# Pieces of eight steps for the read weights, and a doubled planning time for the projections

## The reference

```
xr, gate = split(x @ W_in.T)                    # 1024 + 1024 wide
xc = silu(conv4(xr + t_emb) + b_conv)           # causal, depthwise, 4 taps
xn = layernorm(xc)
Bm, Cm, dt = split(xn @ W_xproj.T, 3)           # 16 + 16 + 16
Ad = 1 + 0.01 * tanh(dt @ W_dt.T + b_dt) * A
Bd = Bm * min(norm(xn), 1)
h  = clip(h * Ad + Bd * xn, -10, 10)            # 16 states x 1024, one step per token
y  = Cm . h + D * xn
out = x + (y * silu(gate)) @ W_out.T
```

## Time and profile before

| what | us |
|---|---|
| median of 3 runs | 6659.12 |
| lowest, highest | 6656.98, 6682.08 |
| profiled execution, its own time | 6651.31 |
| its span from first to last instruction | 6649.5 |
| first `q` to last `q` of the 1024 steps | 3607.1 to 6530.2 |

### The profile page before, as it was taken

The page is one execution under the profiler, slowest core; times in us unless marked ns, Lnnn a source line. Parts: engine busy times, 40 slices in busy tenths (PEclk is TensorE's granted clock), DMA queues, the critical chain, the costliest instruction groups (busy, mean ns, idle before and its releaser), DMA issues. The chain is left out here.

```text
span 6649.5 us, 73076 instructions
## 1 busy us (share of the span) xinstructions
PE 6031.6 (91%) x24000; PEld 2737.8 (41%) x24000; DVE 4565.5 (69%) x5830; ACT 2368.7 (36%) x4476; POOL 3213.6 (48%) x2625
## 2 busy tenths in 40 slices
PE   8999999999999999999965779999999999999997
PEld 4444444444444444444332324444343434444343
DVE  4655655555555556555425988989888888989882
ACT  2444434444444444444524313233232323333110
POOL 1776765767567566665715223424243333424212
PEclk8999999999999999999977989999999999999998
DMA  2223223232231322312123333434344443534433
GB/s 89 79 80 90 86 65 90 66 105 73 73 96 50 108 82 71 99 46 89 41 101 98 79 92 93 134 85 133 97 114 122 111 122 92 136 85 130 104 88 99
DMA packets 411563, 613.28 MB, mean 92 GB/s; under 512 B 58768, under 2 KB 189968, under 8 KB 410672
## 3 DMA queue, kind: packets, MB, share of 16 engines
q1 hardware_dynamic: 374320, 558.24, 30.4%
q10 hardware_dynamic: 36864, 50.38, 3.0%
HBM read 305.31 MB, written 201.38 MB: 76 GB/s over the span
## 5 line engine op out<-in xcount | busy, mean ns | idle before, releaser
L1103 POOL TENSOR_TENSOR acc<-acc,prob 128x512 f32<-128x512 f32 x1536 | 1906.6, 1275 | 960.9 <-PE bank L793 740.8
L1033 DVE TENSOR_REDUCE mx<-bank 128x1 f32<-128x512 f32 x2048 | 1314.9, 684 | 587.1 <-PE bank L763 582.5
L1907 DVE SCALAR_TENSOR_TENSOR g<-xps,bd,g 128x1024 f32<-128x1024 f32 x1024 | 1313.5, 1283 | 236.9 <-PE xps L1669 157.2
L926 ACT ACTIVATE prob<-misc 128x512 f32<-128x512 f32 x1496 | 842.5, 597 | 849.5 <-PE misc L780 688.3
L1669 PE MATMUL xps<-sx,spread 128*128 128x512 f32 x2048 | 899.1, 524 | 249.2 <-DVE g L1907 233.2
L763 PE MATMUL bank<-khat,qhat 96*128 96x512 f32 x2048 | 989.3, 534 | 39.6 <-DVE mx L1033 20.7
L1913 DVE TENSOR_SCALAR g<-g,lim 128x1024 f32<-128x1024 f32 x1024 | 876.3, 856 | 30.0
L780 PE MATMUL misc<-qhat,khat 98*128 98x512 f32 x1679 | 723.9, 461 | 58.4 <-ACT prob L926 42.1
L1669 PEld LDWEIGHTS xps<-sx,spread 128*128 128x128 f32 x2048 | 354.7, 193 | 808.6 <-DVE g L1907 472.1
L1683 PE MATMUL yps<-g,cexp 128*32 128x512 f32 x4096 | 618.7, 631 | 1.2 <-DVE g L1913 0.8
L763 PEld LDWEIGHTS bank<-khat,qhat 96*128 96x128 f32 x2048 | 390.5, 196 | 435.0 <-issue 300.3
(11 more groups left out here) (199 smaller groups left out, 6740.5 us busy)
## 6 DMA issues: line engine op xcount, KB each, us to landing
sx<-scratch_xhl SPq DMA_DIRECT2D x512, 128.0 KB, 5.0
scratch_dx<-dx SPq DMA_DIRECT2D x64, 512.0 KB, 3.0
scratch_xhl<-xhi SPq DMA_DIRECT2D x64, 512.0 KB, 4.6
scratch_xhl<-xn SPq DMA_DIRECT2D x64, 512.0 KB, 4.9
scratch_y<-ysb SPq DMA_DIRECT2D x512, 64.0 KB
dx_t<-scratch_dx SPq DMA_DIRECT2D x59, 512.0 KB, 6.2
y_t<-scratch_y SPq DMA_DIRECT2D x59, 512.0 KB, 4.3
xt_n<-in_x SPq DMA_DIRECT2D x112, 256.0 KB, 2.9
```

Source lines behind the costliest of these rows:

```text
L926: act.activation(to, bank[m][:, 0:QC], ACT.Exp, scale=SCALE).then_inc(sem[f"act_m{m}"], 1)
L1033: dve.tensor_reduce(self.mx2[:, h * TT + qt, c:c + 1], bank[m][:, 0:QC], AX.X, ALU.max).then_inc(sem[f"dve_m{m}"], 1)
L1103: pool.tensor_tensor(self.acc[:, a, h, :], self.acc[:, a, h, :], self.prob[:, (n % 2) * GH + h, :], ALU.add).then_inc(sem["pool_acc"], 1)
L1907: dve.scalar_tensor_tensor(self.g[:, t % 4, :], self.xps[t % 2][:, :], self.bd[:, i % 2, tl:tl + 1], self.g[:, (t - 1) % 4, :], ALU.mult, ...
```

## The change

It has two parts.

Read weights: `out` waits for the piece of eight steps it reads rather than the last piece of the half. A piece is made once the `out` that last read those eight steps has gone. The planner sees 0.65 for a piece and no longer 0.8. Only the first piece of a chunk stays at the end of the rows' lane; the other fifteen have a lane of their own, due from 4 steps ahead of the chunk to 0.84 of it.

Projections: the planner believes 0.9 instead of 0.47 for half a batch's projection.

```diff
-    def expand(i, h):
-        done = (("out", (i - 1) * TOK + (h + 1) * HC - 2),) if i else ()
-        return [item("POOL", 0.8, ("ex", i, h, a), (("d3", i),) + done, [("pool_ex", 1)], port=True) for a in range(HC // 8)]
+    def expand(i, some):
+
+        done = lambda k: (("out", (i - 1) * TOK + 8 * k + 6),) if i else ()
+        return [item("POOL", 0.65, ("ex", i, 8 * k // HC, k % (HC // 8)), (("d3", i),) + done(k), [("pool_ex", 1)], port=True)
+                for k in some]
...
-                    put("PE", 0.47, ("pj", i, hb, bb, q), (("silu", i, hb, CT - 1),), [("pe_m{m}", 1)] if q else [],
+                    put("PE", 0.9, ("pj", i, hb, bb, q), (("silu", i, hb, CT - 1),), [("pe_m{m}", 1)] if q else [],
...
-        return out + expand(i, 0)
+        return out + expand(i, range(1))
...
-                put(t, "PE", 1.0, ("out", t - 1), (("g", t),) + ((("ex", i, h, HC // 8 - 1),) if tl % HC == 1 else ()) + (
+                put(t, "PE", 1.0, ("out", t - 1), (("g", t),) + ((("ex", i, h, tl % HC // 8),) if tl % 8 == 1 else ()) + (
...
-        order.lane(expand(i, 1), t - 1.0, t + 0.25 * TOK)
+        order.lane(expand(i, range(1, TOK // 8)), t - 4.0, t + 0.84 * TOK)
...
-                w.wait_ge(sem["pool_ex"], plan.after("pool_ex", ("ex", t // TOK, t % TOK // self.HC, self.HC // 8 - 1)))
+                w.wait_ge(sem["pool_ex"], plan.after("pool_ex", ("ex", t // TOK, t % TOK // self.HC, t % self.HC // 8)))
...
-                    w.wait_ge(sem["pe_y"], plan.after("pe_y", ("out", (i - 1) * self.TOK + (h + 1) * self.HC - 2)))
+                    w.wait_ge(sem["pe_y"], plan.after("pe_y", ("out", (i - 1) * self.TOK + h * self.HC + 8 * a + 6)))
```

## The result

The changed kernel takes 6680.64 us (median of 20 runs, 6665.93 to 6689.27); the kernel before takes 6659.24 in 20 runs beside it. The ratio is 1.003, 95% interval [1.0023, 1.0037]: slower by 0.3%, a difference that so many runs do tell from none. The forecast was 6631, faster by 28, in a range of 6590 to 6685.

The account below looks back on a forecast made before the run. VectorE and PE alternate in a ring; time can be won only where VectorE idles and PE can feed it. 6651.31 (profiled) - 28 = 6623, that execution being 7.8 us under the median, so 6631; range 6590 to 6685.

Parts of the forecast that it names:

- Part 1a: At steps 39 to 43 and 80 to 82 of a chunk: truer projection time removes waits of `pjo`, 28 us gained.
- Rival 1: At both `pjo` places PE is the limit; waits only move from `proj` to `xps`: 6659, no change, chance 0.23.
- Part 1b: What else the 0.9 moves in the convolution's lane (items due up to 3.5% earlier): nothing, between -6 and +6 us.
- Part 2a: Waits of `out` for read weights, now for one piece: the old wait was always met, so 0.
- Part 2b: Moving the pieces on GpSimd: later rows and possible collisions with `g`, taken as 0, bounds -5 to +54 us.
- Its two mechanisms: Rows' chain ending about 9 us later, under 12 us of cover; late unpaced items colliding with `g`, 0.92 us each.
- rival 3: At the chunk's head the rows' chain becomes the bound, with nine unpaced collisions: 6698, slower, chance 0.15.
- Rival 2: Near the projections the plan is now true and all direct and following waits go: 6591, chance 0.15.
- `pjo` under 10, `xps` up by less than 30, chunks of 370 to 373, `g` at 856: Signs the forecast is right: `pjo`'s wait from 50.3, `q`'s for `xps` from 157.2, chunk times in us, mean `g` in ns.
- wrong if chunks get over 377: Sign that the prediction is wrong: chunks of the changed stage take over 377 us.

Follow-up runs that it names:

- e_dur65: The changed kernel with the convolution's lane ending at 0.65 of the chunk instead of 0.62 and due steps weighted as for 0.47: 6622.7 us, ratio 0.9937.
- e_proj: The kernel before with only the projections' believed time raised from 0.47 to 0.9: 6684.3 us, ratio 1.0044.
- e_wait_only: The kernel before with only the waits of the change, every engine's order kept: 6658.7 us, ratio 0.9997.
- e_read: The changed kernel with the projections' believed time put back to 0.47, leaving only the read weights' part: 6677.4 us, ratio 1.0029.

## Why the prediction was wrong

**Part 1a, taken as a gain of 28 us, is the step that failed.** It read the earlier trace rows as slack: `pjo` waits, no `q` near it does, so TensorE "has the inputs ready". The rows of TensorE at the same steps, which I had not set beside them, were gapless. In the order of before, halving the projections returned all of the 49 us taken away, at both places alike. The direct waits stayed in the changed kernel (53.5), and the claim that the false belief of 0.47 is what makes them was wrong: with the 0.9 VectorE meets the same queue. Where they did go (1.7 us in `e_dur65`), the time did not. Rival 1 named this mechanism and I gave it 0.23; it gave 6659, and misses the rest.

**Part 1b, costed at nothing between -6 and +6, is the missing term.** I bounded the reshuffle by the scatter of chunk lengths, in which the clock of TensorE hardly varied (6.8 to 20.5 us low in each of the six). The 0.9 moved the first projections 7 to 9 us ahead in chunks 1 to 6 (13.9 to 4.6 in the calm one), behind steps in which TensorE idles, and there the clock falls for longer. `e_proj` alone costs 25 us by the medians, and most of it goes with the clock. That the place of the projections is what lengthens the stretches rests on where they begin and on the clocks of the kernels with and without the wider due steps; no run moved the projections and nothing else. No sentence of the prediction looked at the granted clock, though it stood in the rows.

**Part 2a held.** The waits give 0 (`e_wait_only`, 0.9997).

**Part 2b, taken as 0, cost 18 us alone**, inside the bounds of -5 to +54. Its two mechanisms don't carry it. The chain of rows did not become late, and collisions fell over the stage (-8 us in `e_read`), though they rose by 6 us in the last steps of the chunks, so rival 3 did not happen. The cost stands in TensorE's waits (+14 us idle) and those of `q` for `xps` (+28), and in a low stretch of chunk 0. The loss in steps 96 to 126 is the part that every kernel with moved pieces pays (11 us in `e_read`). With the lane's end at 0.65 the pieces and the duration together cost 4 us (`e_dur65`), as other steps give time back.

The two costs do not add up. Alone they are 18 and 25 us, together 21, so behind the moved pieces the 0.9 cost 3 us more (6680.6 against 6677.4, less than these runs can tell).

**Rival 2** (all waits go, 6591) fell with 1a. The lists of signs did their work: of "`pjo` under 10, `xps` up by less than 30, chunks of 370 to 373, `g` at 856" the first and third failed; and "wrong if chunks get over 377" came true in two.

**Open:** why a stretch begins 4 us behind the `q` of step 34 in one chunk and 6 in the next, which decides between 17.1 and 3.4 us; how much of the 10 us that chunk 0 of `e_read` lost is the clock; why the gate's load comes late at step 109; and whether the 14 us by the line through the runs is all cause, since slower runs could also make the clock lower.

## What to carry to other kernels

A wait of a reader for a matmul is slack only if TensorE has a gap before it; set the two timelines side by side before a wait is counted as gain. When an order is moved, compare TensorE's busy time for the same number of instructions. If it rises, look at the granted clock, and try the small matmuls away from the steps in which TensorE waits. Compare clocks over many runs, as one profile can fall either way. A lane's end or a due step is a size to scan, as 3% of a chunk was worth 40 us here and the truer duration nothing.

## What the runs showed of the hardware

- TensorE stayed at the lower clock for 17.1 us while it was busy for 17.03 of them (65 records: projections of 48 columns, transposes and the products `x` and `out` of the steps). The full clock came back 0.7 us after the first product of the output projection began (5979.27). In all seven stretches of 17.1 us this took 0.2 to 0.8 us; each began within the wait of 1.97 us for VectorE or just behind it.
- One program's chunk took 375.3 and 382.0 us in two executions, 6.0 us of it in the ten steps of such a stretch. Runs of the changed kernel spread over 0.35% (6665.93 to 6689.27), with a correlation of -0.76 to their granted clock.
- Eight fp32 matmuls of 48 columns, in two records each, take 1.88 us at the full clock and 3.48 to 3.65 at the lower.
